# Constant rows filled ahead of the first norm as double-width words, first tokens loaded first in halves, a new derived order

## The reference

```python
m = silu(mod) @ w_ada + b_ada            # nine vectors of 256: shift, scale, gate x 3
h = ln(x) * (1 + sc_msa) + sh_msa
qkv = roll(h @ w_qkv + b_qkv, -64)       # windows of 128 tokens
o = roll(softmax(q @ k.T / 4) @ v, 64) @ w_so + b_so
x = x + o * g_msa
x = x + topk_cross_attention(ln(x) * (1 + sc) + sh, context) * g_mca
x = x + swiglu(ln(x) * (1 + sc) + sh) * g_mlp
```

## Time and profile before

| | us |
|---|---|
| median of 3 runs | 2537.3 |
| lowest, highest | 2535.52, 2537.45 |
| the profiled execution | 2540.68 |
| its span | 2539.4 |

### The profile page before, as it was taken

One profiled execution on the slowest core, in us unless ns is written; L12 is line 12 of the kernel. 1 busy time (PEld: TensorE's weight loads), 2 busy tenths in 40 slices (PEclk: granted clock), 3 DMA queues, 4 the chain that ended last, 5 costly groups with the idle time before them and its releaser, 6 DMA issues.

```text
span 2539.4 us, 37005 instructions
## 1 busy us (share of the span) xinstructions
PE 2331.7 (92%) x13127; PEld 1214.5 (48%) x13127; DVE 1686.7 (66%) x5146; ACT 1267.6 (50%) x2434; POOL 384.6 (15%) x407
## 2 busy tenths in 40 slices
PE   6789789978997989999989999998999989999997
PEld 2566345555554545545444455552344433334554
DVE  5666978676235575567867775758886668884563
ACT  2334445443222314455546655645766637776553
POOL 3011444244121110001110010010001010002021
PEclk8899789999998979999999999997999999999999
DMA  4666440000001140001223100042221042110120
GB/s 161 186 153 203 123 142 24 28 22 5 4 9 33 63 78 18 14 14 26 94 86 101 56 18 13 14 150 75 66 50 21 18 131 88 52 41 11 51 71 17
DMA packets 150925, 160.63 MB, mean 63 GB/s; under 512 B 33391, under 2 KB 120259, under 8 KB 150477
## 3 DMA queue, kind: packets, MB, share of 16 engines
q1 hardware_dynamic: 150740, 158.28, 22.0%
HBM read 97.39 MB, written 60.19 MB: 62 GB/s over the span
## 4 chain that ended last, share of the span: by engine, by line
PE 74%; DVE 13%; ACT 3%; DMA 3%; POOL 2%; issue 2%; SPq 1%; ACTq 0%; DVEq 0%; POOLq 0%
PE bank L1224 10%; PE bank L1196 9%; PE bank L1758 9%; PE bank L1171 9%; PE bank L1781 6%; PE bank L1200 4%; PE bank L822 4%; PE bank L2264 4%; PE bank L2444 3%; PE bank L1678 3%; DVE max L1303 2%; PE bank L2266 2%; PE bank L740 2%; PE bank L1034 1%; DVE stats L695 1%
## 5 line engine op out<-in xcount | busy, mean ns | idle before, releaser
L1238 ACT ACTIVATE work<-bank 128x512 f32<-128x512 f32 (+1 forms) x1216 | 687.6, 596 | 404.8 <-PE bank L1200 199.5
L1300 DVE CUSTOM_DVE_ANT_0 bank<-bank,weights 128x512 f32<-128x512 f32 x512 | 347.3, 702 | 121.3 <-PE bank L1171 119.8
L1171 PE MATMUL bank<-k_stack,q_stack 97*128 97x512 bf16 x896 | 354.6, 401 | 35.8 <-DVE max L1303 17.6
L1303 DVE TENSOR_REDUCE max<-bank 128x1 f32<-128x512 f32 x512 | 334.1, 684 | 72.5 <-PE bank L1171 70.0
L1196 PE MATMUL bank<-q_stack,k_stack 99*128 99x512 bf16 x896 | 339.9, 383 | 7.5 <-ACT work L1238 5.8
L1758 PE MATMUL bank<-hT,weights 128*128 128x512 f32 x512 | 256.4, 612 | 9.8 <-ACT work L1808 4.3
L1171 PEld LDWEIGHTS bank<-k_stack,q_stack 97*128 97x128 bf16 x896 | 88.3, 99 | 250.9 <-DVE max L1303 106.7
L1200 PEld LDWEIGHTS bank<-ident_b,weights 128*128 128x128 bf16 x2048 | 157.8, 97 | 102.0 <-issue 8.5
L1781 PE MATMUL bank<-weights,work 128*128 128x256 f32 x768 | 195.8, 384 | 3.5 <-DVE work L1848 3.2
L1200 PE MATMUL bank<-ident_b,weights 128*128 128x128 bf16 x2048 | 198.1, 218 | 0.0
L1781 PEld LDWEIGHTS bank<-weights,work 128*128 128x128 f32 x768 | 140.8, 190 | 67.4 <-issue 29.5
(11 more groups left out here) (241 smaller groups left out, 3611.6 us busy)
## 6 DMA issues: line engine op xcount, KB each, us to landing
q_stack<-parts_q SPq DMA_DIRECT2D x60, 384.0 KB, 4.1
parts_q<-parts SPq DMA_DIRECT2D x46, 384.0 KB, 2.6
k_stack<-parts_k SPq DMA_DIRECT2D x40, 384.0 KB, 4.9
weights<-parts_q SPq DMA_DIRECT2D x36, 384.0 KB, 3.8
parts_q<-parts SPq DMA_DIRECT2D x46, 256.0 KB, 2.9
parts_k<-parts SPq DMA_DIRECT2D x24, 384.0 KB, 2.6
parts_k<-parts SPq DMA_DIRECT2D x24, 256.0 KB, 3.0
weights<-in_L_e_w SPq DMA_DIRECT2D x12, 512.0 KB, 7.5
```

The source lines that it names most:

```text
L1171: m = pe.e.matmul(bank.ap[:, :], self.q(g)[0:MAX_ROW, h, qt * P:(qt + 1) * P], k_stacks[self.key, g].ap[0:MAX_ROW, h, half * BLK:(half + 1 ...
L1238: ac.e.activation(p.ap[0:self.nk, :], banks[self.key, "exp", g, i].ap[0:self.nk, :], ACT.Exp).then_inc(*probs.tick((self.key, g, i)))
L1300: ve.e.tensor_tensor_reduce(bank[:, :], bank[:, :], mask_bias[:, qt, half * BLK:(half + 1) * BLK], 1.0, -3.4e38, ALU.add, ALU.max, to).the ...
L1303: ve.e.tensor_reduce(to, bank[:, :], AX_X, ALU.max).then_inc(*maxima.tick((self.key, g, i)))
```

## The change

- Start loads x[0] directly after the condition vector, in two DMAs of four tiles each, each with a semaphore value of its own; the identity, the columns and the modulation weights follow.
- A function `fill` writes constant bf16 rows as f32 words over half as many elements; the words' values are such that both halves of a word are the bf16 constant. StackRows, QueryRows and KeyRows use it for the stacks of 2 x 1024 columns.
- StackRows stands in front of the first norm, with a step for each fill; the ones beside V and the context rows are a stage of their own, ValueOnes, behind the norm.
- Norm can compute its inverse root in parts: for item 0 in two, one for each half of the tiles, with the guess, the Newton step and the normalized tiles of each part in turn. All other norms keep one part.
- The order strings of all five engines are new over their whole length.

The order strings are cut to their first lines.

```diff
@@ -191,44 +191,44 @@
 DIGITS = "0123456789abcdefghijklmnopqrstuvwxyzABCDEFGHIJKLMNOPQRSTUVWXYZ"
 ORDER = {
     "tensor": (
-        "3b6g112d11fc722121454682j26211h1v1431242849272a2ckb442912241t9n1f24341d166g246e451325b945evc246161412123614366216251"
...
+        "1932243d331bb92122712331269222l2b26451z122h2f262895kb2437341Q921j2c2527712d2621282727354975853214561da12246263b13164"
...
     "vector": (
-        "0g1t21112k3a191m182a129a425131bdd23241924211h35262111174vdj21vm3ad8526226891o24122s5135242414e71c219j1b973c312218191"
...
+        "0L114x441J151114b12161436746i431e53421n365yi95952ce9i318heb168c141a242d8859587721112a113b362z7y398213141122de3122331"
...
     "scalar": (
-        "0Zbi52c61d6d6d2716551h6958iZal964596465641hbZ8k312511k4748355Zl5Aj588ga8i898o8hg62315231fc7bc6e14242722j6787e6419661"
...
+        "0Zgi6414591db419241z541564b4cZak9d45716656zbTk512694b4e8Zo322sf3458f888a7216898o7216h51a14294b2273bc442a17252514de62"
...
     "pool": (
-        "0ZDr5Qb8381ARc6ZfZz8341wRc6ZWZBJZZZZZZZZf54Za73DN3"),
...
+        "0ZUr5Qb8381ARc6ZfZz8341wRc6ZWZBJZZZZZZZZf54Za73DN3"),
...
     "sync": (
-        "0212h0520c110908418408408308208010508810e0r02801g02g018c0881020g1aj01g70g41070g60g0b014M10w01w20Zk10b10Zu10ZZZVk0E01"
...
+        "011060281050510c110908408408608108108128r0r02801801o80880871g0bz51gd1017g01062M06M01010M20Z410a10Zv10ZZC02E01Ec0Ej10"
...
@@ -432,10 +432,13 @@
 
             def sync(self, sp):
                 sp.e.dma_start(condT[:, :, :], a["condT"].rearrange("(c p) b -> p c b", p=P)).then_inc(*ld_cond.tick("condT"))
+                tokens = a["x"][0].rearrange("(t p) c -> p t c", p=P)
+                for bl in range(NB):
+                    at = slice(bl * TPB, (bl + 1) * TPB)
+                    sp.e.dma_start(x[0][:, at, :], tokens[:, at, :]).then_inc(*ld_x[0].tick(("x", bl)))
                 sp.e.dma_start(ident[:, :], a["ident"]).then_inc(*ld_cond.tick("ident"))
                 sp.e.dma_start(cols[:, :], a["cols"]).then_inc(*ld_cond.tick("all"))
                 self.mods.begin(sp)
-                sp.e.dma_start(x[0][:, :, :], a["x"][0].rearrange("(t p) c -> p t c", p=P)).then_inc(*ld_x[0].tick("x"))
                 sp.e.dma_start(wt["L0qkv"], w_src["L0qkv"]).then_inc(*ld_w["L0qkv"].tick("L0qkv"))
                 for p in range(1, 4):
                     self.mods.load(sp, p)
@@ -470,30 +473,47 @@
                 po.e.memset(minus_half[:, :], -0.5).then_inc(*pool_done.tick("minus_half"))
                 yield
 
+        PAIR_OF = {-1.0: -1.0058441162109375, 0.0: 0.0, 1.0: 1.0058441162109375}
+
+        def fill(po, rows, value):
+
+            return po.e.memset(rows.rearrange("p h s -> p (h s)").bitcast(F32), PAIR_OF[value])
+
         class StackRows(Stage):
 
             def pool(self, po):
                 for i, (q, k) in ((2, (window_q, window_k)), (0, (q_buf[0], k_buf[0])), (1, (q_buf[1], k_buf[1]))):
                     po.wait_ge(*pool_done.latest)
-                    po.e.memset(k[BIAS_ROW:STACK, :, :], -1.0).then_inc(*pool_done.tick(("k_rows", i, 0)))
+                    fill(po, k[BIAS_ROW:STACK, :, :], -1.0).then_inc(*pool_done.tick(("k_rows", i, 0)))
+                    yield
                     po.wait_ge(*pool_done["k_rows", i, 0])
                     po.wait_ge(*pool_done.latest)
-                    po.e.memset(k[BIAS_ROW:BIAS_ROW + 1, :, :], 0.0).then_inc(*pool_done.tick(("k_rows", i)))
+                    fill(po, k[BIAS_ROW:BIAS_ROW + 1, :, :], 0.0).then_inc(*pool_done.tick(("k_rows", i)))
+                    yield
                     po.wait_ge(*pool_done.latest)
-                    po.e.memset(q[BIAS_ROW:BIAS_ROW + 1, :, :], 1.0).then_inc(*pool_done.tick(("q_rows", i)))
+                    fill(po, q[BIAS_ROW:BIAS_ROW + 1, :, :], 1.0).then_inc(*pool_done.tick(("q_rows", i)))
+                    yield
+
+        class ValueOnes(Stage):
+
+            def pool(self, po):
                 po.wait_ge(*pool_done.latest)
                 po.e.memset(V[:, :, :, D:DV], 1.0).then_inc(*pool_done.tick("V_ones"))
+                yield
                 po.wait_ge(*pool_done.latest)
                 po.e.memset(V_high[:, :, :, D:DV], 1.0).then_inc(*pool_done.tick("V_high_ones"))
+                yield
                 for b in range(B):
                     po.wait_ge(*pool_done.latest)
                     po.e.memset(Vx[b][:, :, D:DV], 1.0).then_inc(*pool_done.tick(("Vx_ones", b)))
+                    yield
                     po.wait_ge(*pool_done.latest)
                     po.e.memset(kx_stack[b][BIAS_ROW:STACK, :, :], -1.0).then_inc(*pool_done.tick(("kx_rows", b, 0)))
+                    yield
                     po.wait_ge(*pool_done["kx_rows", b, 0])
                     po.wait_ge(*pool_done.latest)
                     po.e.memset(kx_stack[b][BIAS_ROW:BIAS_ROW + 1, :, :], 0.0).then_inc(*pool_done.tick(("kx_rows", b)))
-                yield
+                    yield
 
         class Constants(Stage):
             def sync(self, sp):
@@ -676,12 +696,14 @@
         class Norm(Stage):
 
 
-            def __init__(self, lane, b, name, eps, scale, shift, mods, x_at, free, roll=False, blk=None):
+            def __init__(self, lane, b, name, eps, scale, shift, mods, x_at, free, roll=False, blk=None, roots=1):
                 self.lane, self.b, self.eps, self.scale, self.shift = lane, b, eps, scale, shift
                 self.mods, self.x_at, self.free, self.roll, self.blk = mods, x_at, free, roll, blk
                 self.tiles = tiles_of(blk)
                 self.key = (name, b, blk)
                 self.lead = len(self.tiles) // 2 + 2
+                n = len(self.tiles) // roots
+                self.parts = [self.tiles[k * n:(k + 1) * n] for k in range(roots)]
                 self.z_done = evac if name in ("L2n2", "L3n2") and blk is None else vec
                 self.beats = self.lead + len(self.tiles) + 2
 
@@ -700,24 +722,27 @@
                             ve.e.bn_aggr(mv[b][:, s, :], stats[b][:, s, :]).then_inc(*vec.tick((key, "mean", s)))
                             yield
                         yield
-                lo, hi = self.tiles[0], self.tiles[-1] + 1
-                vec.also((key, "means"), (key, "mean", hi - 1))
-                yield
-                yield from inverse_root(ve, key, rstd[b][:, lo:hi], newton[b][:, 0, lo:hi], newton[b][:, 1, lo:hi])
-                ve.wait_ge(*vec[key, "root"])
-                if self.z_done is evac:
-                    ve.e.scalar_tensor_tensor(out=newton[b][:, 0, lo:hi], in0=mv[b][:, lo:hi, 0], scalar=-1.0, in1=rstd[b][:, lo:hi],
-                                              op0=ALU.mult, op1=ALU.mult).then_inc(*vec.tick((key, "shift")))
-                    yield from rest(1 + len(self.tiles))
-                    return
-                yield
-                for t in self.tiles:
-                    z = work[key, "z", t]
-                    for f in z.free:
-                        ve.wait_ge(*f)
-                    ve.e.tensor_scalar(z.ap[:, 0:C], x[b][:, t, :], mv[b][:, t, 0:1], rstd[b][:, t:t + 1],
-                                       ALU.subtract, ALU.mult).then_inc(*vec.tick((key, "z", t)))
-                    yield
+                for part in self.parts:
+                    lo, hi = part[0], part[-1] + 1
+                    vec.also(((key, lo), "means"), (key, "mean", hi - 1))
+                yield
+                for part in self.parts:
+                    lo, hi = part[0], part[-1] + 1
+                    yield from inverse_root(ve, (key, lo), rstd[b][:, lo:hi], newton[b][:, 0, lo:hi], newton[b][:, 1, lo:hi])
+                    ve.wait_ge(*vec[(key, lo), "root"])
+                    if self.z_done is evac:
+                        ve.e.scalar_tensor_tensor(out=newton[b][:, 0, lo:hi], in0=mv[b][:, lo:hi, 0], scalar=-1.0, in1=rstd[b][:, lo:hi],
+                                                  op0=ALU.mult, op1=ALU.mult).then_inc(*vec.tick((key, "shift")))
+                        yield from rest(1 + len(self.tiles))
+                        return
+                    yield
+                    for t in part:
+                        z = work[key, "z", t]
+                        for f in z.free:
+                            ve.wait_ge(*f)
+                        ve.e.tensor_scalar(z.ap[:, 0:C], x[b][:, t, :], mv[b][:, t, 0:1], rstd[b][:, t:t + 1],
+                                           ALU.subtract, ALU.mult).then_inc(*vec.tick((key, "z", t)))
+                        yield
 
             def tensor(self, pe):
                 key = self.key
@@ -743,10 +768,12 @@
                     yield
 
             def pool(self, po):
-                b, lo, hi = self.b, self.tiles[0], self.tiles[-1] + 1
+                b = self.b
                 yield from rest(len(self.tiles) // 2)
-                root_guess(po, self.key, rstd[b][:, lo:hi], newton[b][:, 0, lo:hi], mv[b][:, lo:hi, 1], self.eps)
-                yield
+                for part in self.parts:
```

(15 more changed lines are left out.)

58 lines of the change are left out of this document (29 added, 29 removed).

## The result

Over four runs each, the time went from 2536.8 to 2475.2 us (median). The ratio is 0.9754, 95% interval 0.9738 to 0.9771, so 61.6 us were gained, where 8.7 were forecast and the range ended at 2511. The profiled executions differ by more, 2540.7 and 2470.3 us (spans 2539.4 and 2468.8). Ratios use undisturbed executions alone; one of fill_first's twelve, at 3373.9 us and a granted clock of 0.645, is left out.

A forecast was written before the change was run, and what follows sets the result against it. TensorE, busy 92% of the span with 74% of the last chain, was taken as the bound. The first projection's start, 36.02 to 27.3 us, gave -8.7 and all else zero: median 2537.3 to 2528.6 us, range 2511 to 2545.

The forecast's parts named there:

- Fills: Nine constant-row fills on POOL, moved to the start as double-width words: 0.94 us each, over by 9.8 us.
- The rival that they aren't cheaper: Front fills cost more than 0.94 us: 2536.6 us at 1.83 each, 2545.3 at 2.8; chance 0.10.
- VectorE at the start: Small operations ahead of the first norm's statistics wait for fills until 10.0 us; statistics to 13.5, first two tiles 15.6.
- TensorE's pieces: Modulation pieces between the first norm's tile turns: 3.57 us after idling, 1.88 after some 4 us of work.
- piece 1: Modulation piece on TensorE after the first two tiles, forecast from 16.3 to 19.9 us.
- the mark: Start of the first projection on TensorE: 27.3 us forecast in place of 36.02, a gain of 8.7.
- my bound of 25: Upper bound on the front's gain, 11 us, if the second guess holds nothing and piece 1 runs at the quick price.
- The rival of a gain absorbed by a lower clock in the projection: Earlier load or lower clock takes 4 us before the window attention: 2532.6 us; chance 0.10.
- Later fills at nothing: Nine later fills of key and query rows get 0.9 us shorter; taken to gain nothing.
- The third queue's loads at nothing: Second item's tokens and context weights loaded earlier in SP's queue: 1.4 us of DMA time, taken as hidden.
- The order: New order strings of all engines, whole kernel: taken as zero, bounded by about 11.6 us a stage either way.
- The rival of an order that gains: New interleaving gains 11.6 us of TensorE's idle time: 2517.0 us; chance 0.14.

The follow-up runs named there:

- fill_first: Kernel before with idle matmuls on TensorE ahead of the first four turns of the top-k stage; 2536.2 us, ratio 0.9991.
- single_width: Changed kernel with the fills as bf16 elements again, 2048 a row; 2484.7 us, ratio 0.9797 against the kernel before.
- new_front_lanes: Changed kernel with its new order only up to the start of the first window attention, old order behind it; lead over the kernel before 21.7 us.
- order_but_sync: Kernel before with the new order strings but the old one for SyncE, which issues nearly all DMAs; 2530.1 us, ratio 0.9962.
- order_only: Kernel before with the new order strings, VectorE's adapted to one root; 2488.0 us, ratio 0.9804.
- the ladder: Changed kernels with the new order up to successive stages' ends, then the old; front edits 7 us, front's order 6, top-k and MLPs 28, two self attentions 16.

## Why the prediction was wrong

- **Fills.** 0.94 us each, over at 9.8, were forecast; 0.95 and 9.86 came. The rival that they aren't cheaper is refuted, and single_width shows what they carry. The Trainium skill, "GPSIMD Engine Reference", section 3.1, led to an estimate of 0.88; the measured 0.95 decides.
- **VectorE at the start.** I let the small operations wait for a whole fill each, up to 10.0. They were stretched to 0.44 and 0.67 us and less, and the statistics, which ran beside the last fill at 0.36 each, weren't held: they started at 8.45. The first tiles were done at 13.2 and not 15.6. This term was 2.4 us too large.
- **TensorE's pieces.** I gave piece 1 3.57 us, the price of an engine that has been idle. It took 1.88, since piece 0 and a turn ran right before it. With this and shorter waits for tiles, the mark came at 22.54 and not 27.3, below even my bound of 25. The rival of a gain absorbed by a lower clock in the projection was the wrong way round: 7.13 us in place of 9.99.
- **Is the front's gain kept?** Yes: 13.5 us at the mark, 13 in new_front_lanes. 8.7 was a third too low, and 7.9 of the 13.5 need the new order of the front, because with the old one the mark is 30.39. Later fills at nothing: nothing contradicts it. The third queue's loads at nothing: no run moves them alone, but order_but_sync shows that this queue's order as a whole is not free.
- **The order.** This is the step that failed: "I take zero for it", bounded by "about 11.6 us for a stage that interleaves badly". Measured are 50 us (order_only); the ladder, on the changed kernel, has 28 in the top-k stage and 16 in two self attentions. The bound was wrong in three ways. It compared slices behind 1000 us only, and never looked at the stretch from 250 to 370 us, where TensorE was idle 26.6 us and had a clock of 0.80. It counted idle time alone, while 36.4 of the 70.6 us between the profiled executions are TensorE's busy time, up to 31 of them by the lower clock; the column of the granted clock stands in the earlier trace rows and I left it out of the sum. And it took TensorE's share of the chain for the whole kernel, though VectorE is busy 83% of the stretch from 250 us, in the stage that gained most. It also left out the DMA queue's order, without which the new order is worth 0.38% and not 1.96. The rival of an order that gains had the right sign, 0.14 of chance and a quarter of the size.
- **The test I set.** I wrote that I am wrong if TensorE's idle time behind 130 us changes by more than 5 us. It fell from 170.8 to 142.3 us, for the same 12601 matmuls.
- **What stays open.** The ladder shows in which stages the order gains, and order_but_sync that the compute strings carry most of the top-k stage. By what waits they do so is open. The projection in one block in the middle of the maxima isn't it: the lead stays at 32.3 to 32.9 us over those turns. That the bias row's load sets the stage's start was read from the traces and agrees with order_but_sync; no run moves that load alone. For the self attentions only the place (16 us) and the dependence on SyncE's order are shown; in the traces TensorE's idle time falls from 31.2 to 21.8 us there, and no single wait holds it. How much of the 36 us of busy time is cause and how much follows from shorter waits isn't settled either; fill_first shows one place where more clock alone was worth nothing.

## What to carry to other kernels

An order of unchanged instructions is an edit of its own. Before it is priced, each stage is to be looked at by TensorE's idle time, its granted clock and the fullest other engine. A bound from idle time alone was too low here; idle time and half the time at the lower clock together are the safer one, though regained clock can be worth nothing. Where an in-order DMA queue feeds the stage, its order has to be derived with the others: the new order without SyncE's part was worth a fifth of the whole (0.38% against 1.96). To find what bounds a stage, add idle work to one engine at a time, and count in the trace how much of it ran. A wait that shrinks is no proof of a gain: follow how much earlier the same instructions start, ahead of the place and behind it.

## What the runs showed of the hardware

A fill on POOL is priced by elements and not by bytes: 0.95 us for 1024 f32 words and 1.83 for 2048 bf16 elements, the same 4096 bytes. One-input VectorE operations beside back-to-back fills took 0.44 to 0.67 us, while normalizing tiles took 1.76 each before; statistics beside a fill kept their 0.36. A lower-clock stretch got 10 us shorter (27.3 to 17.1, fill_first) when 3.6 us of TensorE's waits ahead of it were filled with idle matmuls, and the time stayed the same.
